# Expert tiles of 128 token rows in place of 256 in a gated attention and mixture-of-experts kernel

## The reference, cut to what matters

```
x = x + tanh(g_xattn) * attention(layernorm(x), ctx, ctx)
y = layernorm(x)
logits = y @ Wr + br                        # [4096, 8 experts]
weights = softmax over the top 2 logits     # the others are -inf
h = gelu(y @ W1[e] + b1[e])                 # 256 -> 1024
out = sum over e of weights[:, e] * (h @ W2[e] + b2[e])   # 1024 -> 256
x = x + tanh(g_ffn) * out
```

## Time and profile before

| | |
|---|---|
| median of 3 runs | 983.84 us (979.72 to 990.62) |
| the profiled execution's own time | 979.53 us |
| its span, first to last instruction | 977.8 us |
| mean granted TensorE clock | 0.941 of full |
| PE busy | 887.0 us, 91% |
| DVE / ACT / POOL busy | 605.2 / 444.2 / 252.7 us |

### The profile page before, as it was taken

One profiled execution on the slowest core, in us unless ns is written; L12 is line 12 of the kernel. 1 busy time (PEld: TensorE's weight loads), 2 busy tenths in 40 slices (PEclk: granted clock), 3 DMA queues, 4 the chain that ended last, 5 costly groups with the idle time before them and its releaser, 6 DMA issues. The chain is left out here.

```text
span 977.8 us, 25308 instructions
## 1 busy us (share of the span) xinstructions
PE 887.0 (91%) x7728; PEld 774.3 (79%) x7729; DVE 605.2 (62%) x1521; ACT 444.2 (45%) x962; POOL 252.7 (26%) x229
## 2 busy tenths in 40 slices
PE   4799999999999999999609999999899989999991
PEld 3688888888888888887508898899798979999880
DVE  3468788888688877777645565556456555556550
ACT  2354555555445545554205454455354444454440
POOL 2001233322033232223210223233313222232322
PEclk9799999999799979999658999999999999999996
DMA  7766877767587874767688632333222332332212
GB/s 161 135 128 173 192 192 190 167 177 167 164 190 195 195 187 101 169 178 231 220 314 321 168 61 47 52 57 52 47 45 46 51 54 38 49 54 41 29 23 24
DMA packets 86071, 124.34 MB, mean 127 GB/s; under 512 B 8928, under 2 KB 77664, under 8 KB 81760
## 3 DMA queue, kind: packets, MB, share of 16 engines
q1 hardware_dynamic: 70592, 102.90, 40.6%
q0 software_dynamic: 14304, 19.15, 12.3%
q10 hardware_dynamic: 1088, 1.11, 0.4%
HBM read 55.21 MB, written 42.75 MB: 100 GB/s over the span
## 5 line engine op out<-in xcount | busy, mean ns | idle before, releaser
L1289 PE MATMUL bank<-xh,wts 128*128 128x256 f16 x1872 | 216.6, 277 | 0.0
L1165 POOL DMA_INDIRECT out_rows<-yg,xs x78 | 126.9, 1627 | 346.8 <-ACT yg L1207 202.8
L1305 PE MATMUL bank<-wts,hh 128*128 x1872 | 210.6, 273 | 0.0
L1289 PEld LDWEIGHTS bank<-xh,wts 128*128 x1872 | 186.0, 99 | 23.9 <-issue 0.2
L1305 PEld LDWEIGHTS bank<-wts,hh 128*128 128x128 f16 x1872 | 183.2, 98 | 21.2
L1197 ACT ACTIVATE hf<-bank,b1t,gscale 128x256 f32<-128x256 f32 x312 | 154.8, 561 | 23.9 <-PE bank L1289 22.0
L906 PE MATMUL bank<-va,probs 128*128 128x17 f32 x1024 | 134.8, 265 | 7.6 <-DVE ao L626 7.6
L906 PEld LDWEIGHTS bank<-va,probs 128*128 128x128 f32 x1024 | 128.4, 197 | 10.1 <-DVE ao L626 7.4
L514 ACT ACTIVATE probs<-bank 128x512 f32<-128x512 f32 x128 | 76.5, 598 | 121.4 <-PE bank L891 120.7
L1207 ACT ACTIVATE yg<-yb,xs 128x256 f32<-128x256 f32 x78 | 35.4, 500 | 204.2 <-DVE yb L1246 198.9
L1236 DVE SCALAR_TENSOR_TENSOR hh<-hf,hscale,hh 128x512 f16<-128x512 f32 x156 | 117.2, 751 | 5.6
(11 more groups left out here) (168 smaller groups left out, 1201.9 us busy)
## 6 DMA issues: line engine op xcount, KB each, us to landing
wts<-in_W SPq DMA_DIRECT2D x16, 1024.0 KB, 7.9
split_weights<-wts SPq DMA_DIRECT2D x16, 1024.0 KB, 5.0
wts<-split_weights SPq DMA_DIRECT2D x16, 1024.0 KB
wts<-keys SPq DMA_DIRECT2D x96, 128.0 KB
wts<-queries SPq DMA_DIRECT2D x96, 128.0 KB
xs<-token_rows SPq DMA_DIRECT2D x39, 272.0 KB
xin<-in_x SPq DMA_DIRECT2D x16, 256.0 KB, 4.9
cin<-in_ctx_in SPq DMA_DIRECT2D x16, 256.0 KB, 5.2
```

The lines of the kernel that those rows point to most:

```text
L1165: pool.indirect_dma_start(out=out[:, :], out_offset=bass.IndirectOffsetOnAxis(ap=numbers, axis=0), in_=yg[m % 2][:, half, :], in_offset=No ...
L1289: last = pe.matmul(HB[c // 2][:, c % 2 * TILE:(c % 2 + 1) * TILE], wts[:, bass.ds(expert[1], 1), at:at + P], xh[b][:, xp, k, :], start=q = ...
L1305: last = pe.matmul(YB[b][:, half * D:(half + 1) * D], hh[b][:, hp, c, half * P:(half + 1) * P], wts[:, bass.ds(expert[0], 1), at:at + D], ...
```

## The change

The tiles have 128 rows; there are 71 of them, all written out, with no loop. A tile's first layer has the same 48 matmuls with 128 moving columns in place of 256; its second layer has 24 matmuls of 256 columns in place of 48; 2 transposes in place of 4. The first-layer results of a tile fill two PSUM banks, and there are two such sets. Gelu works on 8 pieces of 128 x 128, the split on two halves of 128 x 512 a tile. There is one scatter-add a tile. Rings are 16 (rows) and 4 (results) deep. The expert number is read once a tile on each engine. The padding writes have 128 rows, and the tile table is made for 71 tiles in place of 128. The order of the products in both layers is changed, so that the three products of one block stand together.

```diff
-TILE = 2 * P
+TILE = P
...
-RING = 8
+RING = 16
+YRING = 4
...
-        eng.dma_start(env["xs_dram"][bass.ds(place, TILE), :].rearrange("(h p) r -> p h r", h=2),
-                      env["padrow"][:, :].unsqueeze(1).to_broadcast([P, 2, ROW])).then_inc(env["pads_in"], 16)
+        eng.dma_start(env["xs_dram"][bass.ds(place, TILE), :],
+                      env["padrow"][:, :]).then_inc(env["pads_in"], 16)
...
-        HB = bank[1:5]
+        HB = [bank[1:3], bank[3:5]]
...
             first = -(-(lo + 1) // RING) * RING
-            rounds = (hi - 3 - first) // RING
+            if hi == MAIN_TILES:
+                first = hi
+            rounds = (hi - 3 - first) // RING if first < hi else 0
             peeled(lo - 2, first)
...
# POOL
-                        for half in range(2):
-                            pool.wait_ge(yg_ready, i * 2 + half + 1)
-                            when(pool, half == 1 or before(i, 1), added[1 - half],
-                                 added_value(i if half == 1 else i - 1))
...
+                        pool.wait_ge(yg_ready, i + 1)
+                        when(pool, before(i, 1), added, added_value(i - 1))
...
# ACT
-                        for quarter in range(4):
-                            act.wait_ge(h_psum, (i + 1) * 4 + quarter + 1)
...
+                        for half in range(2):
+                            act.wait_ge(h_psum, (i + 1) * 2 + half + 1)
...
# TensorE
-                        expert[0] = expert[1] if m > 0 and not isinstance(i, int) else expert_of(pe, i)
+                        expert[0] = expert[1] if m > 0 or isinstance(i, int) else expert_of(pe, i)
...
-                        terms = [(wp, xp, k) for wp, xp in ((0, 0), (0, 1), (1, 0)) for k in range(KC)]
+                        terms = [(wp, xp, k) for k in range(KC) for wp, xp in ((0, 0), (0, 1), (1, 0))]
...
-                                last = pe.matmul(HB[c // 2][:, c % 2 * TILE:(c % 2 + 1) * TILE],
+                                last = pe.matmul(HB[b][c // 4][:, c % 4 * TILE:(c % 4 + 1) * TILE],
                                                  wts[:, bass.ds(expert[1], 1), at:at + P], xh[b][:, xp, k, :],
                                                  start=q == 0, stop=q == 5)
...
-                        for half in range(2):
-                            for q, (hp, wp, c) in enumerate(terms):
-                                if half == 0 and q % 6 == 0:
-                                    pe.wait_ge(split_ready, i * 4 + q // 6 + 1)
-                                at = 4096 + wp * 2048 + c * D
-                                last = pe.matmul(YB[b][:, half * D:(half + 1) * D],
-                                                 hh[b][:, hp, c, half * P:(half + 1) * P],
-                                                 wts[:, bass.ds(expert[0], 1), at:at + D], start=q == 0, stop=q == 23)
+                        for q, (hp, wp, c) in enumerate(terms):
+                            if q % 12 == 0:
+                                pe.wait_ge(split_ready, i * 2 + q // 12 + 1)
+                            at = 4096 + wp * 2048 + c * D
+                            last = pe.matmul(YB[b][:, 0:D], hh[b][:, hp, c, :],
+                                             wts[:, bass.ds(expert[0], 1), at:at + D], start=q == 0, stop=q == 23)
```

More of the change, by code:

```diff
@@ L981, in tile_table @@
     step(dve.tensor_copy(tile_no[:, :], tile_no_int))
[L983 to L998, removed]
+    rows_of_tiles(dve, step, env, 0, MAIN_TILES)
     dve.wait_ge(most_total, 1)
@@ L1071, in pipeline @@
             first = -(-(lo + 1) // RING) * RING
-            rounds = (hi - 3 - first) // RING
+            if hi == MAIN_TILES:
+                first = hi
+            rounds = (hi - 3 - first) // RING if first < hi else 0
             peeled(lo - 2, first)
-            with eng.Fori(0, rounds) as u:
-                for m in range(RING):
-                    it(u * RING + (first + m), m, lambda k: True)
+            if rounds:
+                with eng.Fori(0, rounds) as u:
+                    for m in range(RING):
+                        it(u * RING + (first + m), m, lambda k: True)
             peeled(first + RING * rounds, hi)
@@ L1201, in it @@
                     if there(0):
-                        e = expert_of(act, i)
+                        e = expert[0]
                         act.wait_ge(yb_ready, i + 1)
-                        when(act, before(i, 2), added[1], added_value(i - 2))
-                        for half in range(2):
-                            act.activation(yg[m % 2][:, half, :], yb[m % 2][:, half, :], ACT.Copy,
-                                           scale=xs[m][:, half, bass.ds(e + D, 1)]).then_inc(yg_ready, 1)
+                        when(act, before(i, YRING), added, added_value(i - YRING))
+                        act.activation(yg[m % YRING][:, :], yb[m % YRING][:, :], ACT.Copy,
+                                       scale=xs[m][:, bass.ds(e + D, 1)]).then_inc(yg_ready, 1)
                 all_tiles(act, it)
@@ L1214, in _ @@
                 step = Links(dve, dve_steps)
+                expert = {}
                 def it(i, m, there):
+                    if there(0):
+                        expert[0] = expert[1] if m > 0 or isinstance(i, int) else expert_of(dve, i)
+                    if there(1):
+                        expert[1] = expert_of(dve, i + 1)
                     if there(2):
@@ L1224, in it @@
                     if there(1):
-                        e = expert_of(dve, i + 1)
-                        b = (m + 1) % 2
-                        for quarter in range(4):
-                            c = slice(2 * quarter, 2 * quarter + 2)
-                            dve.wait_ge(gelu_ready, (i + 1) * 4 + quarter + 1)
-                            when(dve, quarter == 0 and before(i + 1, 2), y_psum, i)
+                        e, b = expert[1], (m + 1) % 2
+                        for half in range(2):
+                            c = slice(4 * half, 4 * half + 4)
+                            dve.wait_ge(gelu_ready, (i + 1) * 2 + half + 1)
+                            when(dve, half == 0 and before(i + 1, 2), y_psum, i)
                             high = hh[b][:, 0, c, :].rearrange("p c t -> p (c t)")
-                            full = hf[:, c, :].rearrange("p c t -> p (c t)")
+                            full = hf[b][:, c, :].rearrange("p c t -> p (c t)")
                             step(dve.tensor_scalar(high, full, hscale[:, bass.ds(e, 1)], None, ALU.mult))
@@ L1255, in _ @@
                 step.restart()
-                all_tiles(dve, it)
+                pipeline(dve, it, 0, MAIN_TILES)
+                ties = dve.value_load(mostint[0:1, 0:1], min_val=0, max_val=E)
+                with dve.If(ties > 2):
+                    for lo in range(MAIN_TILES, ALL_TILES, MAIN_TILES):
+                        n = min(MAIN_TILES, ALL_TILES - lo)
+                        step(dve.tensor_scalar(tile_no[:, :], tile_no[:, :], float(MAIN_TILES), None, ALU.add))
+                        rows_of_tiles(dve, step, env, lo, lo + n)
+                    dve.sem_inc(rest_ready, 1)
+                    step.restart()
+                    pipeline(dve, it, MAIN_TILES, ALL_TILES)
             @block.tensor
@@ L1270, in it @@
                         for k in range(KC):
[L1271 to L1274 removed]
+                            last = pe.transpose(XT[:, k * P:(k + 1) * P], xs[(m + 2) % RING][:, k * P:(k + 1) * P],
+                                                ident[:, :])
                         last.then_inc(xT_psum, 1)
```

116 lines of the change are left out of this document (65 added, 51 removed).

## The result

The changed kernel takes 1068.8 us (median of 4 runs, 1068.3 to 1072.1), the kernel before 982.5 (median of 4 beside it): a ratio of 1.087, with a 95% interval of 1.080 to 1.094. It is slower by 86 us. Forecast were 1080 us and a range of 1020 to 1120.

The account below looks back on a forecast made before the run. PE's array bounds the old kernel; its sequencer would bound the new one at 7.65 us a tile. Start 544, 67 tiles of 512.6 us, last two 7.5 and 2.7, end 11.6, and 1.7 around: 1080 us, range 1020 to 1120.

Parts of the forecast that it names:

- the first rival: PE's array sets the second stage's pace at 5.6 us a tile, so the change is faster: 941 us; chance 0.10.
- Sequencer time a tile, 7.65 us: PE's sequencer, second stage: first layer 4.3, second layer 2.1, last matmul 0.05, expert number and waits 1.2 us.
- What the matmul rows would show: On PE, first-layer matmuls start 85 to 95 ns apart, not 55; second-layer ones 109 ns apart.
- The bounds: Sequencer time a tile lies between 7.15 us (operations alone, 124 ns apart) and 8.05 us (pace of the loop's tiles).
- The start: PE waits for the fifth tile's rows to land, some 3 us earlier than before: at 544 (540 to 547).
- The end: After the last matmul, 2.3 us to POOL's last add and 9.3 behind it: 11.6 us.
- Other engines at nothing: ACT at most 5.2 us and DVE at most 6.0 per old tile, POOL 4.7 to 4.9 a tile: covered by 7.65.
- The clock: Rival: holes in PE drop its clock to half for half the time, mean tile 9.2 us, kernel 1186 us; chance 0.05.

## Why the prediction was right

The mechanism was right and was shown by taking it away: with fixed addresses in both layers the changed kernel is 27 us faster than the kernel before (one run beside one), and 11 us over the 941 of the first rival; its fifth tile started 4 us late.

By its steps:

- **Sequencer time a tile, 7.65 us.** Measured 7.46 (second layers at 548.22 and 1048.30, 67 tiles apart). This is the term of the sum that was mis-sized, by 0.19 a tile or 13 us over 68 tiles. The span came out 11.3 us short of the forecast: 13 for this, 0.4 for the start, and 2 the other way for the end. In the tile shown above the first layer took 4.27 for 4.3, the second 2.15 for 2.15; the head, expert number and waits, took 1.0 (804.1 to 805.1) for 1.2, and that is where the 0.19 lies. I had read it off a tile with two reads, from the start of the second one to the first layer.
- **What the matmul rows would show:** 85 to 95 ns forecast, 89 measured; and 5.6 us at the array's pace, 5.64 measured with fixed addresses. The Trainium skill's 81 ns for such pairs (TensorE: Matmul & The Clock Gate, section Back-to-back issue gap) is not borne out here: with fixed addresses they start 56 ns apart over 48 pairs in a row, tile after tile.
- **The bounds.** The lower one, 7.15, took the operations at 124 ns and the matmuls among them at nothing. That is close to what the records show. With the measured head it would be 48 x 0.124 + 1.0 = 7.0; the missing 0.5 us is in the longer distances after every seven or eight operations and in the waits within the layers. The point value needed no such split, because it was read off tiles with the same operations and matmuls.
- **The start,** 544: measured 543.60. That is partly luck: in the traces of the 128-row kernels with the same order of issues it lies between 539.7 and 551.6.
- **The end,** 11.6 us behind the last matmul: measured 13.6 (the last add starts 5.0 behind the last matmul for 2.3, and the span ends 8.6 behind it for 9.3). I let the last add follow its data and forgot that the last two tiles end close together (there is no first layer between them), so that the older add's landing is late.
- **Other engines at nothing:** right. ACT's Gelu is 456 ns for 128 columns and 561 for 256, so ACT's time rose by 70 us, and hides. POOL waited for ACT's result (392 us between 545 and 1040) and not for a landing, as forecast.
- **The clock:** stayed at full in the steady tiles (1.00 from 560 to 1040), with holes in PE of under 0.1 us up to 1000. The rival didn't come.

## What to carry to other kernels

Before cutting matmuls into narrower ones, count what the sequencer does for each of them: in these kernels every distinct block addressed through a register was an operation, for 128 columns as for 256. Whether there is room is seen in how far the sequencer is ahead, not in PE's busy share: if its next read or wait stands behind a full queue there is slack; if its register operations come one after the other, it is the bound, though the profile says 99.6% and the chain of waits names matmuls. Fixed addresses, where a kernel can have them, take the bound away: a tile of 7.46 us became one of 5.64. Here, with the expert known only at run time, the gain was in writing the loop out, at the old tile.

## What was not expected

- Without register operations the sequencer hands over a load and a matmul in 31 ns or less. With them the operations set the pace, 124 ns from one to the next whether one pair or two lie between, and 133 on the mean, where the record of one shows 46.
- A read of the expert number on PE costs 0.69 us of the tile when nothing hides it, and after a jump back it comes on top: 5.38 us of wait where 3.54 stood.
- In the kernel with four more reads PE stands 2.0 to 3.1 us in every tile and the clock falls in some of them: 0.95 granted over 800 to 900, and a tile of the loop in which it falls takes 14.8 to 14.9 us in place of 13.2 to 13.5. With one read more on the changed kernel PE stands 0.6 to 0.7 us a tile, and the clock stays at 1.00.
